# A four-layer graph network on one core: layers 0 and 3 store scanned hidden rows of 128 and make the last linear map per node; table lookups by one-hot products in every second chunk of layer 0 and every third of layer 3

## The reference

```python
h = jnp.maximum(_layernorm(x), 0.0)
# layer 0: W1 is 128x128, W2 is 128x48
t = relu(concatenate([h[dst], h[src], edge_attr_32], axis=1) @ W1 + b1)
x = x + segment_sum(t @ W2 + b2, dst)
...
# layer 3: W1 is 112x128, W2 is 128x128, W3 is 128x48
t = relu(concatenate([h[src], h[dst], edge_attr_16], axis=-1) @ W1 + b1)
t = relu(t @ W2 + b2)
message = t @ W3 + b3
x = x + segment_sum(message, dst) / maximum(count, 1.0)
```

## Time and profile before

| | us |
|---|---|
| median of 3 runs | 7793.15 (7792.11 to 7808.14) |
| the profiled execution | 7796.36 |
| its span, first to last instruction | 7794.6 |
| PE, DVE, ACT, POOL busy in the span | 6659.6, 5210.7, 2085.6, 5823.6 |
| mean granted clock of TensorE (1 is 2.4 GHz) | 0.941 |
| chain that ended last, by engine | POOL 48%, issue 16%, PE 6%, DVE 3% |

### The profile page before, as it was taken

The page is one execution under the profiler, slowest core; times in us unless marked ns, Lnnn a source line. Parts: engine busy times, 40 slices in busy tenths (PEclk is TensorE's granted clock), DMA queues, the critical chain, the costliest instruction groups (busy, mean ns, idle before and its releaser), DMA issues.

```text
span 7794.6 us, 87563 instructions
## 1 busy us (share of the span) xinstructions
PE 6659.6 (85%) x29454; PEld 5473.0 (70%) x29454; DVE 5210.7 (67%) x6271; ACT 2085.6 (27%) x5004; POOL 5823.6 (75%) x6117
## 2 busy tenths in 40 slices
PE   0799999999669999999479999999139999999992
PEld 0688888888557777777367777777127777777771
DVE  6577777777667777777767777777545666666663
ACT  5133333333212222222300000000014444444441
POOL 7777777777777777777767777777777777777776
PEclk9999999999879999999689999999569999999995
DMA  8354544444323333333223333333124444444441
GB/s 321 84 113 112 113 111 113 112 112 113 84 62 83 82 82 88 82 82 82 59 63 74 74 74 77 75 74 74 44 59 98 100 98 98 98 98 99 98 99 42
DMA packets 1063994, 722.05 MB, mean 93 GB/s; under 512 B 583026, under 2 KB 970916, under 8 KB 1063428
## 3 DMA queue, kind: packets, MB, share of 16 engines
q1 hardware_dynamic: 850448, 510.81, 23.7%
q0 software_dynamic: 197008, 163.26, 13.7%
q10 hardware_dynamic: 16100, 42.39, 1.4%
HBM read 478.38 MB, written 237.49 MB: 92 GB/s over the span
## 4 chain that ended last, share of the span: by engine, by line
POOL 48%; issue 16%; PE 6%; DVE 3%; DMA 1%; ACT 0%; POOLq 0%; DVEq 0%
POOL G L683 42%; POOL R L702 5%; PE pOdd L905 4%; PE pRows L905 1%; POOL first_rows L644 1%; DVE onehot L1288 1%; DVE S L1337 1%; PE pRows L1002 0%; PE pOdd L897 0%; DVE G L1300 0%; ACT G L828 0%; DMA G<-table,e_dst 0%; DMA G<-table,idx 0%; DVE pT L1322 0%; DMA prefix<-O 0%
## 5 line engine op out<-in xcount | busy, mean ns | idle before, releaser
L683 POOL DMA_INDIRECT G<-table,idx x2923 | 2758.3, 944 | 891.0 <-issue 878.2
L683 POOL DMA_INDIRECT G<-table,e_dst x2497 | 2362.8, 946 | 790.7 <-issue 753.7
L1223 DVE TENSOR_TENSOR_SCAN K<-mask_f,K,pT 48x512 f32<-48x512 bf16 x782 | 1005.4, 1286 | 1242.5 <-PE pT L970 1117.0
L1002 PEld LDWEIGHTS pRows<-w,S 128*128 128x128 f32 x6256 | 1573.9, 324 | 304.4 <-issue 179.2
L905 PE MATMUL pOdd<-h_high,onehot 128*128 128x480 f32 (+1 forms) x3880 | 1519.5, 392 | 0.0
L905 PE MATMUL pOdd<-h_low,onehot 128*128 128x480 f32 (+1 forms) x3880 | 1489.6, 384 | 0.0
L1002 PE MATMUL pRows<-w,S 128*128 128x48 f32 x6256 | 1445.3, 374 | 2.1 <-ACT O L838 0.5
L905 PE MATMUL pRows<-h_high,onehot 128*128 128x480 f32 (+1 forms) x2430 | 952.6, 392 | 85.1 <-DVE h_low L1076 85.1
L905 PE MATMUL pRows<-h_low,onehot 128*128 128x480 f32 (+1 forms) x2430 | 920.4, 379 | 0.0
L1288 DVE TENSOR_TENSOR onehot<-mask_f,pEven 128x2560 fp32r<-128x2560 f32 (+1 forms) x390 | 892.1, 2288 | 19.4 <-DMA mask_f<-pick_row 19.4
L905 PEld LDWEIGHTS pOdd<-h_high,onehot 128*128 128x128 f32 x3880 | 749.8, 193 | 128.5 <-issue 3.9
(11 more groups left out here) (203 smaller groups left out, 8666.6 us busy)
## 6 DMA issues: line engine op xcount, KB each, us to landing
mask_f<-same_row SPq DMA_DIRECT2D x392, 256.0 KB, 3.3
prefix<-O SPq DMA_DIRECT2D x194, 512.0 KB, 3.6
G<-first_rows SPq DMA_DIRECT2D x784, 96.0 KB
prefix<-O SPq DMA_DIRECT2D x390, 192.0 KB
G<-table,idx POOLq DMA_INDIRECT x2923
G<-table,e_dst POOLq DMA_INDIRECT x2497
first_rows<-zeros ACTq DMA_DIRECT2D x14, 2688.0 KB, 15.5
K<-in_ea_dram SPq DMA_DIRECT2D x588, 64.0 KB
```

Source lines behind the costliest of these rows:

```text
L683: pool.indirect_dma_start(rows[:, slot, j, 0:widths[l]], None, table[l], bass.IndirectOffsetOnAxis(ap=at[:, n, j:j + 1], axis=0))\
L1002: last = pe.matmul(o, s[:, :, j], (w2_0 if l == 0 else w3_3)[:, :], start=True, stop=True)
L1223: dve.tensor_tensor_scan(K[r, c.slot, :], mask_of(c, r), pT[c.slot % 2][r, :], K[r, (c.slot - 1) % RING, CHUNK - 1:CHUNK], ALU.mult, ALU.add)\
```

## The change

In layers 0 and 3 the scanned rows of 128 are no longer multiplied by the last weight on every edge. `turn_rows` transposes them, ACT copies 512 columns a chunk instead of 192, and `prefix` holds rows of 128 floats (512 KB for a pair of chunks instead of 192 KB). The ring of stored rows has 4 slots instead of 8. At the layer end the 98 reads bring rows of 128, and for each group of 7 blocks PE transposes them (`multiply_rows`), ACT copies them back (`copy_hidden`) and PE multiplies them by the last weight. Picks come in every second chunk of layer 0 (190) and every third of layer 3 (126), with shorter lags. In layer 3 `layer_2`, the second ReLU, the scan and `turn_rows` stand one step later, and `layer_1` has one bank. The first sums of layer 1's picks are placed between the groups of layer 0's end.

```diff
-EDGE_PICK_CYCLE = {0: 3, 3: 6}
-EDGE_PICK_LAG = {0: 5, 3: 6}
+ROW_RING = 4
+EDGE_PICK_CYCLE = {0: 2, 3: 3}
+EDGE_PICK_LAG = {0: 4, 3: 5}
...
-    row_width = [D, WIDE, WIDE, D]
+    row_width = [HID, WIDE, WIDE, HID]
...
+        TURN_BANKS = ((0, TJ), (TJ, NODE_BLOCKS))
-        edge_sum = {0: [pH2[1], pH2[0]], 3: [pO[1]]}
+        edge_sum = {0: [pH2[1], pH2[0]], 3: [pO[1], pH1[1]]}
+        first_bank = {0: pH1, 3: [pH1[0]]}
+        node_rows = pH1[0][:, 0:NODE_BLOCKS * D].rearrange("p (b d) -> p b d", d=D)
...
-                    W = TJ * widths[l]
-                    act.activation(O[:, c.slot, 0:W], rows_bank[l][c.n % len(rows_bank[l])][:, 0:W], ACT.Copy).then_inc(rows_copied[l], 1)
+                    act.activation(O_hidden[:, c.n % ROW_RING, :], rows_bank[l][c.n % len(rows_bank[l])][:, :], ACT.Copy)\
+                       .then_inc(rows_copied[l], 1)
...
+                def copy_hidden(v, q):
+                    before_q = 2 * (TURNED_BEFORE[v] + q)
+                    for i, (first, stop) in enumerate(TURN_BANKS):
+                        act.wait_ge(hidden_turned, before_q + i + 1)
+                        act.activation(R_turned[:, q % 2, first:stop, :],
+                                       pT[i][:, 0:(stop - first) * P].rearrange("k (b p) -> k b p", p=P), ACT.Copy)\
+                           .then_inc(hidden_copied, 1)
...
+            def multiply_rows(v, q):
+                before_q, s = 2 * (TURNED_BEFORE[v] + q), q % 2
+                pe.wait_ge(last_rows_in[v][s], (q // 2 + 1) * 16 * NODE_BLOCKS)
...
+                    for k in range(first, stop):
+                        last = pe.transpose(pT[i][:, (k - first) * P:(k - first + 1) * P], R_hidden[:, s, k, :], ident[:, :])
...
+                        last = pe.matmul(node_rows[:, k, :], R_turned[:, s, k, :], (w2_0 if v == 1 else w3_3)[:, :],
+                                         start=True, stop=True)
...
-                        o = rows_bank[l][c.n % len(rows_bank[l])][:, j * w:(j + 1) * w]
-                        last = pe.matmul(o, s[:, :, j], (w2_0 if l == 0 else w3_3)[:, :], start=True, stop=True)
+                        o = rows_bank[l][c.n % len(rows_bank[l])][:, j * HID:(j + 1) * HID]
+                        last = pe.transpose(o, s[:, :, j], ident[:, :])
...
-                stages = {0: [(0, transpose_rows), (1, layer_1), (3, make_rows), (0, sum_edge_pick)],
-                          3: [(0, transpose_rows), (1, layer_1), (3, make_rows), (1, layer_2), (0, sum_edge_pick)]}[l]
+                stages = {0: [(0, transpose_rows), (1, layer_1), (3, turn_rows), (0, sum_edge_pick)],
+                          3: [(0, transpose_rows), (1, layer_1), (4, turn_rows), (2, layer_2), (0, sum_edge_pick)]}[l]
                 by_chunks(stages, NCH)
+                for q in range(NQ):
+                    multiply_rows(l + 1, q)
```

More of the change, by code:

```diff
@@ L568, in store @@
                     sp.wait_ge(rows_copied[l], c.n + 1)
-                    W, first = TJ * D, c.slot // 2 * 2
-                    sp.dma_start(rows_view[c.n // 2 * 2:c.n + 1, :, :].rearrange("c p w -> p c w"),
-                                 O[:, first:c.slot + 1, 0:W]).then_inc(rows_stored[c.pair], 16)
+                    first = c.n // 2 * 2
+                    sp.dma_start(rows_view[first:c.n + 1, :, :].rearrange("c p w -> p c w"),
+                                 O_hidden[:, first % ROW_RING:c.n % ROW_RING + 1, :]).then_inc(rows_stored[c.pair], 16)
                 if l == 2:
@@ L696, in _ @@
                 for q in range(NQ):
-                    if q >= 2:
+                    if q >= 2 and l in MLP:
+                        pool.wait_ge(hidden_turned, 2 * (TURNED_BEFORE[v] + q - 1))
+                    elif q >= 2:
                         pool.wait_ge(last_rows_used[v], q - 1)
@@ L847, in _ @@
                 for q in range(NQ):
+                    if l in MLP:
+                        copy_hidden(v, q)
                     if v == 2:
@@ L921, in sum_picks @@
             def sum_picks(l):
[L923 to L934, removed]
+                if l == 2:
                     pe.wait_ge(split_made, SPLIT_BEFORE[l] + 1)
-                for d in range(first, DUOS):
+                for d in range(2, DUOS):
                     pe.wait_ge(picks_marked[l], d + 1 - FIRST_DUO[l])
@@ L941, in sum_picks, with sum_first_picks @@
                     last.then_inc(picks_summed[l], 1)
+            def multiply_rows(v, q):
+                before_q, s = 2 * (TURNED_BEFORE[v] + q), q % 2
+                pe.wait_ge(last_rows_in[v][s], (q // 2 + 1) * 16 * NODE_BLOCKS)
+                if q:
+                    pe.wait_ge(hidden_copied, before_q)
+                for i, (first, stop) in enumerate(TURN_BANKS):
+                    for k in range(first, stop):
+                        last = pe.transpose(pT[i][:, (k - first) * P:(k - first + 1) * P], R_hidden[:, s, k, :], ident[:, :])
+                    last.then_inc(hidden_turned, 1)
+                if q:
+                    pe.wait_ge(last_rows_used[v], q)
+                for i, (first, stop) in enumerate(TURN_BANKS):
+                    pe.wait_ge(hidden_copied, before_q + i + 1)
+                    for k in range(first, stop):
+                        last = pe.matmul(node_rows[:, k, :], R_turned[:, s, k, :], (w2_0 if v == 1 else w3_3)[:, :],
+                                         start=True, stop=True)
+                last.then_inc(nodes_multiplied, 1)
+            def sum_first_picks(blocks):
+                for g in range(PICK_GROUPS):
+                    if -(-min((g + 1) * SPAN, B) // NODE_BLOCKS) != blocks:
+                        continue
+                    if g == 0:
+                        pe.wait_ge(picks_marked[1], 2)
+                    pe.wait_ge(split_made, SPLIT_BEFORE[1] + blocks)
+                    for d in range(2):
+                        if g == 0:
+                            hide_unchosen_of(d)
+                        last = add_rows(d, g)
+                    if g == PICK_GROUPS - 1:
+                        last.then_inc(picks_summed[1], 2)
             for l in range(4):
@@ L956, in _ @@
                         for g in range(PICK_GROUPS):
-                            last = add_group(out, edge_onehot[i % 2], g)
+                            last = add_group(out, edge_onehot[0][i % 2], g)
                         last.then_inc(edges_summed, 1)
@@ L990, in layer_2, with turn_rows @@
                       .then_inc(hidden2[l], 1)
-                def make_rows(c, l=l):
+                def turn_rows(c, l=l):
                     pe.wait_ge(scanned[l], c.n + 1)
```

57 lines of the change are left out of this document (37 added, 20 removed).

## The result

The changed kernel takes 7696.81 us (median of 4 runs, 7695.74 to 7712.45) against 7792.63 us (4 runs, 7791.38 to 7808.14) for the kernel before: a ratio of 0.9877, 95% interval 0.9859 to 0.9895. It is faster by 96 us. The forecast was 30 us faster and its range ended at 7700, so the direction was right and the time lies 3 us outside the range, where rival (a) had put it (7695). The profiled execution is the slowest of the four, 7712.45 us with a span of 7710.7; the median is 16 us lower.

A forecast was written before the change was run, and what follows sets the result against it. POOL's gathers were taken to bound layer 3, with PE nearly tied in layer 0, where PE and DVE would then decide. Layer 0 +37, layer 3 -79, ends and DMA +12: -30 us, 7763 against the median; range 7700 to 7815.

The forecast's parts named there:

- rival (a): Layers 0 and 3: transposing loads don't pay for the stride, T from 0.44 to 0.72; 7695 us at 0.44; chance 0.2.
- T: Time of a chunk's four transposes of strided `S` on PE, taken as 0.80 us.
- the sum for layer 0: 190 pick cycles at 9.31 us against 1720 us before, +49; less 12 at the end: +37 us.
- 8.51 + T: Layer 0's cycle of two chunks, with `layer_1` waiting for DVE's scan: 9.31 us at T = 0.80.
- the wait for the last gathers: Near layer 0's end PE waited 6.8 us for gathers; this was to go, taken as -12 us.
- -79: Layer 3: 63 gathers less at 1.248 us each on POOL, if PE keeps up.
- 0.82: Layer 3: T in us up to which PE stays under POOL's 13.73 per three chunks; beyond, each 0.1 costs 39 us.
- rival (b): Layers 0 and 3: strided load and moving columns don't overlap, T above 0.88; 8080 us at 1.36; chance 0.14.
- Layer ends: Added transposes, copies and passes behind the last group's landing: about 5.5 us at each end, +11 us.
- The start: More pick numbers lengthen DVE's setup by 0 to 5 us, hidden by PE's 11.6 us wait for the scatter.
- The wider stores: Stores grow by 320 KB a pair, landing in 3.6 us: nothing in the loops, +1 us at both layer ends together.
- rival (c): Layers 0 and 3: the clock falls; 5% of 3600 us at 1.2 GHz gives +125 us, 7888; chance 0.04.

The follow-up runs named there:

- e2: The kernel before, with `make_rows` products reading contiguous slices of `S` instead of every fourth float: 7787.95 us, 0.9994 of the kernel before.
- e1: The changed kernel with `turn_rows` transposing contiguous slices of `S` instead of every fourth float: 7692.85 us, 0.9869 of the kernel before.
- e6: The changed kernel with every transpose of `S` made twice: 7791.8 us, 0.9999 of the kernel before.
- e5: The kernel before with only the new picks of layer 0 (every second chunk, lag 4): 8055.14 us, 1.0334 of the kernel before.
- e8: e3 with every transpose of `S` made four times: 8438.73 us, 1.0828 of the kernel before.
- e3: The changed kernel with DVE's scan placed ahead of marking the pick in layer 0: 7638.47 us, 0.9801 of the kernel before.
- e7: The kernel before with DVE's scan placed ahead of marking the pick in layer 0: 7793.45 us, 1.0001 of the kernel before.
- e0: The changed kernel measured once more, unaltered, as the measure for runs beside it: 7701.2 us, 0.9879 of the kernel before.
- e4: The changed kernel with the old picks (every third chunk in layer 0, every sixth in layer 3): 7795.35 us, 1.0001 of the kernel before.

## Why the prediction was off, point by point

**The price of the strided transposes, T, is the step that failed.** The prediction read that the eight passes of L1002 do not follow the clock and that the strided load is what they wait for. e2 confirms that: contiguous, they take half. The next step, "the transposes load the same slices", carried the price to another form of instruction, and there it doesn't hold: T is 0.39 in one step of layer 0's cycle, 0.47 in the other and in layer 3, not 0.80. e1 puts the whole stride at 0.03 us for four. That is rival (a), whose only row in favour, the four transposes of `G` at 0.44, was the nearest one in form (transposes against the identity), while the row taken was the nearest in data. The Trainium skill (SBUF — State Buffer, section "Door 1: The DMA port swizzle") speaks of a penalty for accesses that go to a new 16-byte line each time. For the loads the trace agrees (329 against 192 ns for a product, 202 against 141 for a transpose), but in the time of four transposes the penalty nearly vanishes (0.39 against 0.36 us). Why a transpose's load pays less for the stride than a product's (61 against 137 ns) no run shows.

In the sum for layer 0, T stands once a cycle, for the step with the wait, where it measures 0.39. The sum falls by 190 x 0.41 = 78 us with it; the miss was 66, and the paragraph on the range says what makes up the rest.

**The loop between PE and DVE in layer 0 was right.** Cycles of two chunks, by the prediction's terms and as measured in steady stretches:

| kernel | T | limit by the terms | cycle measured |
|---|---|---|---|
| change | 0.39 in the step with the wait | scan, 8.51 + T = 8.90 | 9.02 |
| e6 | 0.87 in the step with the wait | scan, 8.51 + T = 9.38 | 9.50 |
| e5 | 1.67 on average | PE, 7.13 + 2T = 10.47 | 10.48 |
| e8 | 1.88 on average | PE, 7.13 + 2T = 10.89 | 10.91 |
| e3 | 0.43 on average | POOL, 7 x 1.248 = 8.74 | 8.74 |

The scan's limit is 0.12 too low both times. The wait itself was sized well: `layer_1` starts 5.51 us behind the transposes of the step before, against 5.49 in the sum (the scan ends 0.09 later than taken, at 5.36, and `layer_1` follows it by 0.15 instead of 0.22). The rest is that a `layer_1` that waited takes 0.93 us to the next start, not 0.86, and that the ten passes take 2.19, not 2.16. The prediction named this limit and that POOL's 8.74 would be missed by it, but gave no price for removing it; e3 does, about 60 us of time.

Layer 0 as a whole: 190 x 9.02 = 1714 us, against 1714 for 126 x 13.60 before. The rest of the layer (chunks without a pick, the two ends) fell from 46 to 26 us, 6 of them for two chunks fewer without a pick. That leaves 14 us, close to the 12 that were taken for the wait for the last gathers. No run took these 14 us apart.

**Layer 3: -73 us in the profiled execution, -78.6 in e3's, where -79 was forecast.** The term is right, the threshold beside it was not. By e8 PE needs 126 x 10.98 + 12 x 2.16 + 390T = 1409 + 390T us for the layer, which meets POOL's 1788 us at T = 0.97. e6 stood just under it, at 1409 + 372 = 1781. The prediction's 0.82 came from a step cost 0.08 too high in each chunk, a pick about 0.06 too high, and from leaving out the 12 chunks without a pick, in which PE catches up. With T on the expected side this cost nothing, but rival (b) was priced too high by it.

**Layer ends: +11 was forecast, some +2 to +3 us came.** The chain behind the last landing is as foreseen. At the end of layer 3 it takes 5.1 us from the first of seven transposes to the first sum on DVE (5.5 forecast), and DVE's last sum ends 10.5 us behind the issue of POOL's last read (L716) instead of 5.1.

```profile
7697.92 0.95 POOL L716 DMA_INDIRECT R_hidden<-prefix,last_edge  x1 [0.30 <-issue]
...
7700.62 1.75 PE L966 MATMUL pT<-ident,R_hidden 128*128 128x128 f32 x7 [3.75 <-DMA R_hidden<-prefix,last_edge]
7701.77 1.13 ACT L860 ACTIVATE R_turned<-pT 128x512 f32<-128x512 f32 x2 [7.70 <-PE pT L966]
...
7702.51 3.19 PE L973 MATMUL pEven<-w,R_turned 128*128 128x48 f32 x14
7705.74 0.51 DVE L1532 TENSOR_TENSOR u<-pEven,inv_count 128x336 f32<-128x336 f32 x1 [6.16 <-PE pEven L973]
...
7707.92 0.51 DVE L1539 TENSOR_TENSOR x<-x,u 128x336 f32<-128x336 f32 x1
```

In the kernel before:

```profile
7784.34 0.94 POOL L702 DMA_INDIRECT R<-prefix,last_edge  x1 [0.30 <-issue]
...
7788.90 0.51 DVE L1480 TENSOR_TENSOR x<-x,u 128x336 f32<-128x336 f32 x1
```

What the sum lacked is that not all of it shows. The program ends when every engine has reached its end. In the four traces with the old ends (before, e2, e5, e7) POOL reaches it 10.04 us behind the issue of its last read, 2.9 to 3.0 us after SP, which waits for the output to land. In the changed kernel SP is there 12.5 us behind that read, and POOL's closing semaphore follows at once. So at the end of layer 3 the longer chain fills the 2.9 us in which the kernel before waited for POOL, and 2.5 us are left of it. The 98 reads are also issued in less time: 125.0 to 125.4 us instead of 127.2 to 127.6 at layer 0's end, and about 1 us less at layer 3's. At layer 0's end the first read also comes 11.0 to 11.5 us behind the last transposes of `G` instead of 12.8.

Whole ends, from the last transposes of `G`, need several traces, as single ones differ by as much as the effect. Layer 0's, up to the first gather of layer 1, takes 150.1 to 150.7 us with the old end and strided products (before, e5, e7) and 150.8 to 152.2 in the change, e0, e1, e3, e4 and e6. Layer 3's, up to the last instruction, takes 153.1, 149.5 and 149.5 us against 148.8 to 152.1, so there the difference is lost in the spread. The table's -2.3 us for it comes from the kernel before's 153.1. The table's +6.3 between the layers is another matter: 5 us of it lie between layer 1's first gather and layer 3's first transposes, in work that the change hardly touches. e0's profiled execution has them too, those of e1, e3, e4 and e6 don't. In the change and e0 the profiled execution is the slowest one, 13 to 16 us above the median. The parts here are readings of traces; no experiment took them apart.

**The start: nothing was forecast, about +4 us came.** The wait for `first_rows` does not hide it, because it is behind POOL's scatter, and the scatter itself takes longer:

```profile
315.25 1.93 PE L1019 MATMUL pT<-ident,G 128*112 128x128 f32 x8 [14.02 <-DMA G<-first_rows]
```

PE's first transposes come at 315.3 instead of 310.0 us here, after 14.0 us of waiting instead of 11.6. Over all traces the start follows the number of picks: 309.4 to 312.0 us in the four with the old number (before, e2, e4, e7), 312.6 in e5 (64 more), 314.5 to 315.3 in the others (127 more). The scatter's longest instruction goes the same way and hardly varies otherwise: 5.93 to 5.94, 6.67, and 7.39 to 7.40 us. The scatter as a whole takes 144.7 to 145.9 us, 146.6, and 148.5 to 149.0. The cause was looked up in the traces, not tried by itself. The prediction's mistake was to take a wait of PE for cover of a delay that lies upstream of the same wait.

**What held.** The wider stores stay hidden, and land in 3.2 us:

```profile
prefix<-O_hidden SPq DMA_DIRECT2D x390, 512.0 KB, 3.2
```

The clock stays at 2.4 GHz in both layers (granted 1.00 and 0.99), so rival (c) did not come about. The Trainium skill (TensorE: Matmul & The Clock Gate, section "Part 4: PE-mode transpose") says that transposes don't count as busy for the clock in the way that products do. In this kernel, with eight of them a chunk beside 0.86 us of real products in layer 0 and 1.72 in layer 3 and the picks, no drop is to be seen, not even in e8 with 16 transposes of `S` a chunk (granted 1.00 in both layers). The granted clock was lower only where PE waits more for gathers: 0.95 in layer 3 (6200 to 7400 us) of e4, with transposes, and 0.95 in the same stretch of e2, with products. No run here tells the two apart further.

**The range.** Rival (a) had been given a chance of 0.2 and the time 7695, but the range ended at 7700, so it cut off the very end that this rival's own working gave. At T = 0.39 the prediction's sum is 7763 - 78 = 7685, 12 us below the result. The cycle 0.12 us longer (+23) and the start (+4) stand against the ends (9 us of the forecast 12 did not come) and the rest of layer 0 (-2), which gives 7701 against 7697 measured. So rival (a)'s 7695 was right in its mechanism, but that it came within 2 us is luck: its T of 0.44 stands 0.05 too high, worth 10 us, and so makes up for most of those 12.

## What to carry to other kernels

A price read from one form of instruction (a two-pass float32 product with a strided stationary operand) doesn't pass over to another form on the same data: take the row nearest in form as an end at least as likely, and let the range reach to it. When an edit puts two DVE operations into one step, look which of the step's outputs another engine waits for, and place that operation ahead of the rest; here it is one line and worth about 60 us. A wait hides a new delay only if the delay does not lie on the way to what is waited for.

## What the runs showed of the hardware that was not expected

- A strided weight load (every fourth float32) takes 329 ns (median) for a product and 202 ns for a transpose, against 192 and 141 contiguous; four products lose 0.73 to 0.85 us by it, four transposes 0.03.
- Transposes of 128 by 128 from strided slices follow one another by about 0.12 us, in runs of 16 (1.84 to 1.92 us, each slice four times) as in runs of 4 (0.39 to 0.47).
- POOL's issue of an indirect DMA can be longer where a DVE operation lies beside it. At layer 0's end all 26 issues of over 1.0 us in the kernel before and all 23 in the change (up to 1.27 us against 0.94) have one beside them and none of the 24 without one is long, though about 50 with one stay short. The longest of the first scatter lasts 7.40 us instead of 5.94 in the kernel whose pick setup on DVE is longer.
- POOL reaches the end of its program 10.04 us behind the issue of its last indirect DMA (four traces), so work on other engines behind the last read is partly hidden by it.
- A wait that an instruction has for several semaphores was put down to ACT's copy in the change and to DVE's scan in e6 and in two thirds of the cases in e1, with the same code around it; the experiment that moved the scan said which one decides.
